# Second mixture of a four-layer network: the choice of experts spread by DMA and multiplied on GpSimd, and the fourth attention's keys projected there

## The reference

```python
x = x + tanh(g_xattn[0]) * L0_attention(layernorm(x), ctx)
x = x + tanh(g_ffn[0])   * L0_mixture(layernorm(x))
x = x + tanh(g_xattn[1]) * L1_mlstm(layernorm(x), ctx)
x = x + tanh(g_ffn[1])   * L1_mixture(layernorm(x))        # changed
x = x + tanh(g_xattn[2]) * L2_perceiver_attention(ctx, layernorm(x))
x = x + tanh(g_ffn[2])   * L2_mixture(layernorm(x))
x = x + tanh(g_xattn[3]) * L3_topk_attention(layernorm(x), ctx)   # changed
x = x + tanh(g_ffn[3])   * L3_block(layernorm(x))

# L1_mixture: 8 experts of 64 hidden units, 2 chosen per token, 1 shared expert of 128
logits = xf @ gate_w.T + lb_bias
topw, topi = top_k(sigmoid(logits), 2);  topw = topw / (topw.sum(-1) + 1e-8)
for e in range(8):
    m = topi == e;  wmean = (topw * m).sum() / max(m.sum(), 1)
    out += where(m.any(-1), (silu(xf @ gw[e].T) * (xf @ uw[e].T)) @ dw[e].T * wmean, 0)
out += (silu(xf @ sg.T) * (xf @ su.T)) @ sd.T

# L3_topk_attention: 16 heads of 8, keys from the context, 32 largest scores kept
q = split_heads(query @ Wq.T);  k = split_heads(ctx @ Wk.T);  v = split_heads(ctx)
scores = q @ k.T * 8 ** -0.5
w = softmax(where(scores >= top_k(scores, 32)[0][..., -1:], scores, -inf))
```

## Time and profile before

| what | us |
|---|---|
| timed runs (3) | 3163.74, 3176.8, 3179.08; median 3176.8 |
| the profiled execution, its time | 3163.17 |
| its span, first to last instruction | 3161.4 |
| second routing, first to last copy on DVE | 926.66 to 944.35 |
| second mixture, until the next stage's first DVE step | 944.9 to 1082.73 |
| fourth attention, first search to last | 1814.64 to 2663 |

### The profile page before, as it was taken

The page is one execution under the profiler, slowest core; times in us unless marked ns, Lnnn a source line. Parts: engine busy times, 40 slices in busy tenths (PEclk is TensorE's granted clock), DMA queues, the critical chain, the costliest instruction groups (busy, mean ns, idle before and its releaser), DMA issues. The chain is left out here.

```text
span 3161.4 us, 70427 instructions
## 1 busy us (share of the span) xinstructions
PE 2849.1 (90%) x21764; PEld 2239.6 (71%) x21764; DVE 2057.4 (65%) x8023; ACT 1813.2 (57%) x5287; POOL 1387.8 (44%) x1689
## 2 busy tenths in 40 slices
PE   7999969977979899999999989999999986694998
PEld 5888844425754588888888778888888874583776
DVE  5554546664564466666655299999999997685332
ACT  5777734434532366666665577788878763251332
POOL 2112237743531043434333267777777775451000
PEclk9999989988989999999999999999999975795999
DMA  3000033415740022112110000000000000001000
GB/s 112 6 6 6 4 82 80 77 57 180 263 154 0 13 58 56 53 53 53 54 56 30 6 6 7 6 6 6 6 6 6 6 31 1 7 18 31 0 0 27
DMA packets 89603, 128.68 MB, mean 41 GB/s; under 512 B 9648, under 2 KB 41920, under 8 KB 88896
## 3 DMA queue, kind: packets, MB, share of 16 engines
q1 hardware_dynamic: 89424, 126.75, 13.9%
HBM read 88.65 MB, written 37.95 MB: 40 GB/s over the span
## 5 line engine op out<-in xcount | busy, mean ns | idle before, releaser
L1790 POOL TENSOR_TENSOR l2a_probs<-l2a_probs,l2a_inv 128x1024 f32<-128x1024 f32 x128 | 242.3, 1893 | 371.9 <-DVE l2a_inv L1956 371.8
L1901 ACT ACTIVATE l2a_probs<-l2a_s_ps,l2a_nm 128x256 f32<-128x256 f32 x512 | 236.1, 472 | 200.3 <-DVE l2a_nm L1932 200.3
L2769 DVE MAX8 l3a_top<-l3a_work 128x8 f32<-128x128 f32 x1536 | 314.6, 279 | 0.0
L2549 PEld LDWEIGHTS l3a_l2o_ps<-net_arena 128*128 128x128 f32 x2016 | 269.6, 219 | 62.0 <-issue 36.6
L2549 PE MATMUL l3a_l2o_ps<-net_arena 128*128 128x128 f32 x2016 | 281.1, 306 | 27.9 <-ACT net_l1f_gate L2625 27.9
L2410 POOL TENSOR_SCALAR l3a_above<-l3a_score,l3a_top 128x128 f32<-128x128 f32 x512 | 298.8, 602 | 16.4 <-DVE l3a_work L2771 6.8
L2771 DVE MATCH_REPLACE8 l3a_work<-l3a_top,l3a_work 128x128 f32<-128x128 f32 x1024 | 269.2, 277 | 0.0
L2537 PE MATMUL l3a_l2h_ps<-net_cols,net_arena 128*128 (+1 forms) x1024 | 248.6, 386 | 3.0 <-ACT net_arena L2662 1.7
L2662 ACT ACTIVATE net_arena<-l3a_l2h_ps,net_l2f_b 128x256 f32<-128x256 f32 x512 | 211.8, 485 | 43.1 <-PE l3a_l2h_ps L2537 39.7
L699 ACT ACTIVATE l0a_probs<-l0a_score_ps,l0a_nm 128x128 f32<-128x128 f32 x512 | 179.6, 381 | 73.7 <-DVE l0a_nm L748 73.7
L2537 PEld LDWEIGHTS l3a_l2h_ps<-net_cols,net_arena 128*128 128x128 f32 x1024 | 184.7, 191 | 51.2 <-issue 20.6
(11 more groups left out here) (526 smaller groups left out, 7158.3 us busy)
## 6 DMA issues: line engine op xcount, KB each, us to landing
kv_ahead<-l1a_kept SPq DMA_DIRECT2D x128, 256.0 KB, 2.8
l0f_code<-code_rows SPq DMA_DIRECT2D x32, 512.0 KB, 10.8
l2a_kT<-kv_ahead SPq DMA_DIRECT2D x64, 256.0 KB, 2.6
l2a_v<-kv_ahead SPq DMA_DIRECT2D x64, 256.0 KB, 2.6
l1a_shift<-neg_top SPq DMA_DIRECT2D x16, 512.0 KB, 5.1
net_x<-x SPq DMA_DIRECT2D x4, 512.0 KB, 6.5
l0a_c_in<-ctxT SPq DMA_DIRECT2D x32, 64.0 KB, 1.8
net_arena<-L_w1T SPq DMA_DIRECT2D x1, 2048.0 KB
```

Source lines behind the costliest of these rows:

```text
L1790: pool.tensor_tensor(p[:, :, :], p[:, :, :], per_row(inv[c % 2][a][:, :, :].rearrange("p i o -> p (i o)"), KV), ALU.mult).then_inc(scaled, 1)
L1901: act.activation(probs[c % 2][a][:, 2 * i + odd, :], s_ps[a][odd][:, i * KV:(i + 1) * KV], ACT.Exp, bias=nm[c % 2][a][:, i, odd:odd + 1], ...
L2549: ins = pe.matmul(output_bank(u, x)[:, at:at + D], hidden[2 * x + n][:, i, j * P:(j + 1) * P], w2[:, expert(u, 2 * x + n), i, :], start=(i ...
L2769: ins = dve.max(t[:, step // 2, h, :], src)
```

## The change

The mask goes by another road. In the routing the transposes start as soon as the mask is there, six groups before the product for the sums and two after. DVE and ACT copy alternate groups to `rows` in fp32, and SP stores them to DRAM (`mask_code`) in two halves. In the mixture SP loads for each pair the two rows, each spread over 64 partitions by the load (`chosen`, a ring of 4), and POOL multiplies the gate by it. PE's mask product and DVE's second multiply are gone. `hidden` has two buffers and `gate` three; the output of a group stands behind step 1 of the next group, and its addition behind step 2.

PE gets the keys of all 32 tiles to project in this stage, 4 tiles ahead of the first group and then one tile after each pair step; ACT copies each tile's result, SP stores it to DRAM (`keys_ahead`). The context, transposed, lies in `net_rows` since the stage `n1a`.

The fourth attention loads each tile's keys (256 KB) from there straight into one of two buffers `kT`. The steps `keys` and `take_keys` are gone, and on PE the first two `hide` steps now stand ahead of the second `output`.

```diff
 def l1_route(nc, k):
+            @block.sync
+            def _(sp):
+                for half in range(2):
+                    cols = slice(half * NB // 2 * P, (half + 1) * NB // 2 * P)
+                    sp.wait_ge(used, NG // 4 * (half + 1))
+                    sp.wait_ge(act_used, NG // 4 * (half + 1))
+                    sp.dma_start(k.mask_code[:, cols], rows[:, cols]).then_inc(k.mask_out, 16)
...
             def _(pe):
+                pe.wait_ge(mask_ready, 1)
+                for g in range(TURNS):
+                    turn(g)
                 pe.wait_ge(part_ready, 1)
                 pe.matmul(sum_ps[:, 0:2 * E], k.ones[:, :], part[:, :, :].rearrange("p a e -> p (a e)"),
                           start=True, stop=True).then_inc(summed, 1)
...
+                for g in range(TURNS, NG):
+                    turn(g)
 def l1_mixture(nc, k):
+                def load(i):
+                    g, c = i // PAIRS, i % PAIRS
+                    if i >= RING:
+                        sp.wait_ge(masked, i - RING + 1)
+                    for n in two:
+                        sp.dma_start(chosen[i % RING][64 * n:64 * n + 64, :],
+                                     k.mask_code[2 * c + n, g * BANK:(g + 1) * BANK].partition_broadcast(64)
+                                     ).then_inc(chosen_in[i % RING], 16)
+                sp.wait_ge(k.mask_out, 32)
+                for i in range(RING):
+                    load(i)
+                for i in range(NG * PAIRS):
+                    keys.keep_one(sp, i)
+                    if i + RING < NG * PAIRS:
+                        load(i + RING)
...
+                        pool.wait_ge(chosen_in[i % RING], 32 * (i // RING + 1))
+                        pool.wait_ge(silu_done, n + 1)
+                        pool.tensor_tensor(gate[n % 3][:, :], gate[n % 3][:, :], chosen[i % RING][:, :], ALU.mult
+                                           ).then_inc(masked, 1)
...
+                for i in range(PAIRS):
+                    keys.project(pe, i)
+                for g in range(NG):
+                    for c in range(NC):
+                        layers(g, c)
+                        if c < PAIRS and g + 1 < NG:
+                            keys.project(pe, (g + 1) * PAIRS + c)
+                        if c == 1 and g:
+                            output(g - 1)
+                output(NG - 1)
 def l3_attention(nc, k):
-        k_in = [s.sb(f"k_in{i}", [P, P]) for i in two]
-        qT, kT = s.sb("qT", [P, P]), s.sb("kT", [P, Q4, P])
+        qT, kT = s.sb("qT", [P, P]), [s.sb(f"kT{i}", [P, Q4, P]) for i in two]
...
-                schedule(pe, [(for_part(output, 0), 1 - AHEAD), (keys, -1), (for_part(output, 1), 1 - AHEAD),
-                              (for_part(hide, 0), -AHEAD), (for_part(hide, 1), -AHEAD), (for_part(turn_probs, 0), 2),
+                schedule(pe, [(for_part(output, 0), 1 - AHEAD), (for_part(hide, 0), -AHEAD), (for_part(hide, 1), -AHEAD),
+                              (for_part(output, 1), 1 - AHEAD), (for_part(turn_probs, 0), 2),
...
-                               (for_part(exps, 2), 1), (take_keys, -1), (for_part(exps, 3), 1),
+                               (for_part(exps, 2), 1), (for_part(exps, 3), 1),
```

More of the change, by code:

```diff
@@ L1642, in _ @@
+                for i in range(PAIRS):
+                    keys.project(pe, i)
+                for g in range(NG):
+                    for c in range(NC):
[5 more added lines that the diff above has]
+                output(NG - 1)
             @block.scalar
             def _(act):
[L1644 to L1652 removed]
+                for i in range(PAIRS):
+                    keys.take(act, i)
@@ L1654, in _ @@
+                for g in range(NG):
+                    for c in range(NC):
+                        n = g * NC + c
+                        act.wait_ge(g_mm, n + 1)
+                        if n >= 3:
+                            act.wait_ge(multiplied, n - 2)
+                        act.activation(gate[n % 3][:, :], g_ps[n % 2][:, :], ACT.Silu).then_inc(silu_done, 1)
+                        if c < PAIRS and g + 1 < NG:
+                            keys.take(act, (g + 1) * PAIRS + c)
             @block.vector
@@ new lines, in _ @@
+                for g in range(NG):
+                    for c in range(NC):
+                        n = g * NC + c
+                        dve.wait_ge(u_mm, n + 1)
+                        if c < PAIRS:
+                            dve.wait_ge(masked, g * PAIRS + c + 1)
+                        else:
+                            dve.wait_ge(silu_done, n + 1)
+                        if c == 0 and g >= 2:
+                            dve.wait_ge(y_mm, g - 1)
+                        dve.tensor_tensor(hidden[g % 2][:, c, :], u_ps[n % 2][:, :], gate[n % 3][:, :], ALU.mult
+                                          ).then_inc(multiplied, 1)
+                        if c == 2 and g:
+                            add(g - 1)
```

205 lines of the change are left out of this document (86 added, 119 removed).

## The result

The changed kernel takes 3135.97 us (median of four runs, 3129.90 to 3150.51) where the kernel before took 3174.28 beside it: a ratio of 0.9899, 95% interval 0.9875 to 0.9922, so 32 us less (25 to 40); the two medians by themselves lie 38 us apart. The prediction was 3159 us, 17.8 us less, and a lower end of 3140: the direction and the places are right, the gain is nearly twice what was forecast.

What follows compares the result with a forecast made beforehand. In the fourth attention PE, a little slower than VectorE's floor, sets the pace; in the mixture PE is the bound. Terms -24 - 1.5 + 7.7 = -17.8 us, so 3159 us from a median of 3176.8; range 3140 to 3178.

Steps and rivals of the forecast that it cites:

- the term was -24: Fourth attention, 25 tiles: VectorE becomes the bound and most of its wait for PE comes back, -24 us.
- The term was -1.5: Start of the fourth attention: the removed keys and the moved hide steps count there once, -1.5 us.
- +7.7 forecast: Second routing and mixture: a longer mixture, +13.1 us, less PE's earlier start, -5.4, makes +7.7 us.
- 5 x 1.92: Mixture: PE's five times 1.92 us of pair work in a new group of 17.83 us.
- nothing, at most +4: Mixture: the ring of kept-key buffers, emptied by stores on SP, costs nothing, at most +4 us.
- 144.8: Mixture: PE's new length of 144.8 us, eight groups plus 2.2 of stalls and last wait, against 131.7 before.
- The -5.4 for PE's early start: Mixture: PE starts near 943.4 instead of 948.76, since keys wait for neither scaling nor masks, -5.4 us.
- +1.9 more: Mixture's start: added cost of 1.9 us if PE, with less idle time before it, does not keep full clock.
- Rival 1: Fourth attention: PE and ACT still set the pace, total -5 us, 3172 us; chance 0.28.
- Rival 2: Mixture: the broadcast loads of the choice land late, +30 us, total +12.6, 3189 us; chance 0.10.
- The walk of one tile: Fourth attention: following one tile's steps with all edits, PE's loop shortens by a mean 1.3 us, to 25.5.
- the lower bound beside it: Fourth attention: the smallest gain, -12 us, if only ACT's 0.48 us a tile comes through.

Runs made afterwards that it cites:

- e4: The changed kernel with eight buffers for kept keys instead of four; ratio 0.9884 to the kernel before.
- e12: The changed kernel with eight buffers for kept keys, the same as e4, timed again; ratio 0.9875 to the kernel before.
- e6: The changed kernel with PE's old order in the fourth attention, both outputs ahead of the first two hide steps; ratio 1.0012 to the kernel before.
- e9: The changed kernel with PE's key work put back in the fourth attention, its result unread and no ACT copy; ratio 0.9949 to the kernel before.
- e10: The changed kernel with an unread ACT copy of 128x512 elements per tile put back in the fourth attention; ratio 0.9980 to the kernel before.
- e3: The changed kernel with the fourth attention of the kernel before, so keys are projected and stored but never read; ratio 1.0024 to the kernel before.
- e7: The kernel before with only the new order, the first two hide steps ahead of the second output; ratio 0.9958 to the kernel before.
- e15: Second profiled execution of e9 (changed kernel, PE's key work back); its 25 tiles took 658.7 us.
- e13: Second profiled execution of e10 (changed kernel, ACT's copy back); 3157.3 us.
- e14: Third profiled execution of e10 (changed kernel, ACT's copy back); 3171.8 us.
- e1: The kernel before, unchanged, in a second profiled execution; 3173.4 us.

## Why the prediction was wrong in size

**Where the gain is: right.** The fourth attention was PE's to pace and is VectorE's now; the wait of `divide` fell to 1.7 to 4.3 us (about 3 forecast) and usual tiles take 25.4 to 25.8. 25 tiles gave -27.0 (671.9 as the mean of two, 644.8 of three) where the term was -24: the 3.4 us kept back for clock and a lead to be built up were too many by 3.

**The start of the stage: mis-sized.** The term was -1.5. From the stage's start to the first search were 68.1 us before and 63.5 after, and to the first `divide` 143.6 and 138.1 to 139.0: -5. The prediction counted the keys and the move once. Up to the first search PE is busy 59.21 us where it was 61.38, and idle 4.3 where it was 6.7: both fell, and by which steps was not followed.

**Routing and mixture: +7.7 forecast, +4.2 measured** (156.4 to 160.6). Two steps of it failed and cancelled in part. "5 x 1.92" took the gate and up products of a pair up to the mask product; they take 1.72 without it, so a group is 16.62, not 17.83, 9.7 us less in eight groups. Against that "nothing, at most +4" for the ring was too low: it costs 4 to 8 us (e4, e12), of which 4 to 6 are PE standing idle. With the ring out of the way the sum comes out: 144.8 - 9.7 = 135.1 us from PE's first to its last product, and e12 has 135.0. The -5.4 for PE's early start was -6.1. PE kept its clock there in the three executions of the changed kernel (the first keys take 3.70 us start to start for 32 instructions, as fast as later ones), but e4, e6, e9 and e10, with the same start, began at 0.50 for some 5 us, four of the twelve executions with keys in the mixture. The prediction's condition for "+1.9 more" is met in some executions and not in others.

**The sum.** -27.0 - 5 + 4.2 = -28 against -17.8 forecast; 29 by the profiles from routing to end, 30 and 32 by the timings. The miss of 10 is three terms that are off by 3 to 3.5 us each and all to the same side. From the 3159 us of the forecast to the median of 3136 are 23 us; the other 13 are no term of the sum but the scatter of single executions (the medians lie 38 us apart where the profiles have 28, and the base was 3174 and not 3177). The lower end of the range was the single term of -24 on the lowest run, so it left no room for that. Rival 1 (PE, ACT and the clock keep the pace) is wrong: the clock did fall, to 0.92 (the prediction took less than that as a sign against it), but the pace had passed to VectorE. Rival 2 is wrong: the choice lands after 3.1 us per 128 KB, and GpSimd never waits for it.

**The mechanism: right in sum, wrong in its parts.** The walk of one tile took all three edits together and was near (1.3 us a tile forecast, 27.0/25 = 1.1 measured, down to VectorE's floor). The step that failed is the lower bound beside it: -12, since "only ACT's 0.48 a tile comes through". With ACT's copy and PE's keys gone and the wait for `take_y` left, nothing comes through (e6). A part of the edits is not worth its share of the sum. What the runs show are three things that each hold the tile above VectorE's 25.6 us, close to one another:

- the second output waits for `take_y`; with the old order it holds the tile at the same 26.8 us with keys or without (e6, e3);
- PE's own work with the keys in it, in the tiles whose mean clock falls to about 0.86 (e7, e9, e15);
- ScalarE's list up to the gelu, for which `hide` waits, with the copy in it (e10, e13, e14).

Any one of the three left in place holds the 25 tiles at 657 to 670 us; only without all three are they 642 to 647. Removing the second and third brings 2, no more than the executions differ (e6 against before), the first alone 6 (e7), removing all three 27. That much is shown; by which instructions each of the three loops back to VectorE was not followed in the trace, and why e10, e13 and e14 differ among themselves by 12 us stays open. They have 2, 6 and 7 tiles over 27 us, and a granted clock of 0.94, 0.93 and 0.92.

A rule of the Trainium skill bears on this (TensorE: Matmul & The Clock Gate, A second HAM failure mode): it tells of a kernel with bf16 products, cycling through PSUM banks, whose short idles between groups made the clock swing. Carried over to this kernel it would make e6, with 40 us of such waits, the one with the lowest clock. Its 25 tiles have 0.94, the changed kernel with 0.4 us of them has 0.92 and 0.93: the trace does not bear it out.

## What to carry to other kernels

When one engine is 5% under the bound and several others wait on each other in a ring, ask of each removed piece of work whether it stood inside a wait: the keys here stood in the wait for `take_y`, so taking them away brought nothing until the wait itself was moved. Savings in such a ring neither add nor can be read one by one; price all edits together against the floor of the next engine, and undo each alone to see which of them hold. And a ring of buffers emptied by DMA has to be sized by the whole way round (store issued behind other loads, 3.2 us to land), since the engine that fills it holds up all that is queued behind it: four buffers cost 4 to 8 us here, and with eight the wait is gone.

## What was not expected of the hardware

The same code up to the second routing takes 926.1 to 940.5 us. Most of the difference is PE's clock in two short feed-forward stages. The first of them, in the profiled execution of before and in e1 (windows as above):

```profile
408.10:424.30 16.20, 14.24 (x120) 13.61 (x120) 6.48 (x28) 10.33 (x24) 6.47 (x4) 0.96 0.48 131
```

```profile
408.60:433.10 24.50, 22.46 (x120) 21.98 (x120) 6.47 (x29) 10.89 (x24) 6.47 (x4) 0.61 0.32 87
```

The same 120 products take 14.24 us at a granted clock of 0.96 and 22.46 at 0.61; the second stage takes 16.7 us at 0.81 and 19.9 at 0.67. Together that is 11.5 of the 12.7 us between these two. Of 17 profiled executions five started the routing by 927 us, five between 932 and 936, and seven from 939 us on. A single execution of this kernel is therefore only good to 14 us, nearly half of what the change is worth; stages are the better measure.

VectorE's product kept its time with GpSimd at work beside it in the same stretch (line, work, count | busy us, mean ns):

```profile
L1673 POOL TENSOR_TENSOR l1f_gate<-l1f_gate,l1f_chosen 128x512 f32<-128x512 f32 x32 | 40.5, 1266 | 116.1 <-ACT l1f_gate L1727 116.1
L1757 DVE TENSOR_TENSOR l1f_hidden<-l1f_u_ps,l1f_gate 128x512 f32<-128x512 f32 x40 | 27.6, 691 | 97.7 <-POOL l1f_gate L1673 84.3 <-ACT l1f_gate L1727 13.4
```

691 ns, against 692 before, and GpSimd's product of the same size at 1266.
